# Four places for the last head's values, and a reordered lead-in with split gates in the experts

## The reference

```python
# cross attention, block 1
q = (inputs_q @ Wq).reshape(b, sq, H, HD) * (1.0 / np.sqrt(HD))      # H, HD = 16, 128
k = (inputs_kv @ Wk).reshape(b, skv, H, HD)                          # skv = 4096
v = (inputs_kv @ Wv).reshape(b, skv, H, HD)
attn = jax.nn.softmax(jnp.einsum('bqhd,bkhd->bhqk', q, k), axis=-1)
ctx = jnp.einsum('bhqk,bkhd->bqhd', attn, v).reshape(b, sq, H * HD)
return ctx @ Wo
# experts, block 6: E, K, F, C = 64, 8, 192, 64
probs = jax.nn.softmax(x @ router_w.T, axis=-1)
wts, idx = jax.lax.top_k(probs, K)
wts = wts / jnp.sum(wts, axis=-1, keepdims=True)
# each token goes to its 8 experts, at most 64 tokens an expert (xg: E x C x D)
h = jax.nn.silu(jnp.einsum('ecd,efd->ecf', xg, w1)) * jnp.einsum('ecd,efd->ecf', xg, v1)
y = jnp.einsum('ecf,efd->ecd', h, w2)
# out[token] = sum over its experts of y[expert, place] * weight
```

## Time and profile before

| | |
|---|---|
| median of 3 runs | 1778.88 us (1778.22 to 1780.69) |
| the profiled execution | 1774.9 us, its span 1772.9 us |
| PE busy | 1704.4 us (96%) |
| DVE, ACT, POOL busy | 1088.1 (61%), 693.3 (39%), 96.4 (5%) |
| the cross attention's last head | about 1164 to 1205 us |
| the experts' lead-in, the loop | about 1510 to 1546, then to the end |

### The profile page before, as it was taken

How to read it: one execution, slowest core, us unless ns; L and a number is a source line. 1 busy time by engine, 2 the same in 40 slices (tenths; PEclk the granted TensorE clock), 3 DMA queues, 4 the chain that set the end, 5 groups by cost and what they waited for, 6 DMA issues and landing times.

```text
span 1772.9 us, 23791 instructions
## 1 busy us (share of the span) xinstructions
PE 1704.4 (96%) x9438; PEld 1343.0 (76%) x9438; DVE 1088.1 (61%) x1738; ACT 693.3 (39%) x937; POOL 96.4 (5%) x177
## 2 busy tenths in 40 slices
PE   8998999999999999999999999978899999899998
PEld 7887888887888888788888788876577466554544
DVE  4446777777677777777777788965538315333333
ACT  4334444445444444444444555542213212212121
POOL 0000000000000000000000010010000000000000
PEclk9999999999999999999999999999999999999999
DMA  6755544445455454454454522252104181488880
GB/s 220 207 166 155 131 131 131 126 131 149 121 132 143 121 137 123 140 143 119 131 136 125 132 96 88 86 192 94 49 1 190 48 356 81 102 307 324 306 323 33
DMA packets 114733, 262.55 MB, mean 148 GB/s; under 512 B 6656, under 2 KB 76480, under 8 KB 108480
## 3 DMA queue, kind: packets, MB, share of 16 engines
q1 hardware_dynamic: 96192, 193.93, 35.5%
q0 software_dynamic: 18432, 67.12, 12.6%
HBM read 193.35 MB, written 67.67 MB: 147 GB/s over the span
## 4 chain that ended last, share of the span: by engine, by line
PE 64%; issue 24%; DVE 5%; DMA 3%; POOL 2%; ACT 1%; SPq 0%; POOLq 0%; DVEq 0%; ACTq 0%
PE bank L41 16%; PE bank L392 14%; PE bank L364 10%; PE bank L405 5%; PE bank L1712 5%; PE bank L1410 3%; PE bank L1733 2%; PE bank L1732 2%; PE bank L138 2%; PE bank L1741 2%; POOL v_back L867 1%; DMA v_dram<-v_out 1%; PE bank L1019 1%; DMA slot_all<-slots_dram 1%; PE bank L430 1%
## 5 line engine op out<-in xcount | busy, mean ns | idle before, releaser
L714 DVE TENSOR_TENSOR e_lo<-S,e_hi 128x1024 fp32r<-128x1024 f32 x128 | 156.6, 1223 | 94.1 <-ACT e_hi L547 93.8
L364 PE MATMUL bank<-cT_hi,wk_hi 128*128 128x512 f32 x512 | 205.6, 402 | 0.0
L392 PE MATMUL bank<-wv_hi,cT_hi 128*128 128x512 f32 x512 | 199.9, 390 | 3.5 <-DVE wv_lo L651 3.5
L364 PE MATMUL bank<-cT_hi,wk_lo 128*128 128x512 f32 x512 | 200.5, 392 | 0.0
L392 PE MATMUL bank<-wv_hi,cT_lo 128*128 128x512 f32 x512 | 199.4, 390 | 0.0
L364 PE MATMUL bank<-cT_lo,wk_hi 128*128 128x512 f32 x512 | 199.2, 389 | 0.0
L392 PE MATMUL bank<-wv_lo,cT_hi 128*128 128x512 f32 x512 | 199.2, 389 | 0.0
L538 ACT ACTIVATE S<-S 128x1024 f32<-128x1024 f32 x128 | 135.6, 1059 | 157.9 <-DVE S L694 157.8
L547 ACT CAST e_hi<-S 128x1024 fp32r<-128x1024 f32 x128 | 134.7, 1052 | 152.3 <-PE bank L405 142.7
L707 DVE TENSOR_TENSOR esum<-esum,S 128x512 f32<-128x512 f32 x210 | 145.1, 691 | 71.9 <-ACT S L538 68.3
L405 PE MATMUL bank<-e_hi,v_back 128*128 128x256 f32 x896 | 170.6, 288 | 12.2 <-DMA v_back<-v_dram 4.3
(11 more groups left out here) (265 smaller groups left out, 2899.8 us busy)
## 6 DMA issues: line engine op xcount, KB each, us to landing
w<-in_w_moe SPq DMA_DIRECT2D x32, 2304.0 KB, 8.5
v_dram<-v_out SPq DMA_DIRECT2D x112, 512.0 KB, 4.6
v_back<-v_dram POOLq DMA_DIRECT2D x112, 512.0 KB, 5.0
v_dram<-v_back SPq DMA_DIRECT2D x16, 512.0 KB, 3.9
v_late<-v_dram POOLq DMA_DIRECT2D x16, 512.0 KB, 3.5
ctx_nat<-in_ctx SPq DMA_DIRECT2D x8, 1024.0 KB, 4.6
ctx_raw<-in_ctxT SPq DMA_DIRECT2D x7, 1024.0 KB, 8.0
l_w_qkv<-in_l_wqkv SPq DMA_DIRECT2D x6, 1024.0 KB, 6.0
```

Source lines behind the costliest of these rows:

```text
L364: t = e.matmul(banks[b][:], l, r, start=(c == 0 and m == 0), stop=(c == DT - 1 and m == 2))
L392: t = e.matmul(banks[b][:], l, r, start=(c == 0 and m == 0), stop=(c == DT - 1 and m == 2))
L714: e.tensor_tensor(lo[:], Sj, hi[:].bitcast(F32), ALU.subtract).then_inc(e_split, 1)
```

## The change

In the last head (n from 120 on, `TAIL`) the values have four places: `v_back`, `v_late`, `v_tail0` (over the spare key tiles `k2_hi` and `k2_lo`) and `v_tail1` (over `wk_hi` and `wk_lo`), with a semaphore each. POOL issues rounds 1, 2 and 3 of that head together when head 14 is weighed, and later ones when the round four before is over. In the experts `slot` is turned before the first gathers; `xn_hi` and `xn_lo` are made before the logits are moved; `slotT` is copied before the gate weights are computed; `slot_all` is read in two pieces, four pairs first; and the gate weights are held as two float32r parts (`gate_parts`), so that a gate product has four columns in float32r instead of two in float32, and DVE adds the two halves when it moves the gates out of PSUM.

```diff
@@ -180,6 +180,10 @@
 
         ones_r, = place(WORK + 4 * (KVT * T + D), ("ones_r", [P, P], F32R))
 
+        TAIL = NH - NCH
+        v_tail0, = place(WV_PLACE + 4 * CT * 2 * XHD, ("v_tail0", [P, CT, 2, XHD], F32R))
+        v_tail1, = place(WORK + 4 * (KVT * T + D + DT * P), ("v_tail1", [P, CT, 2, XHD], F32R))
...
-        v_in = sems("v_in0 v_in1")
+        v_in = sems("v_in0 v_in1 v_in2 v_in3")
...
@@ -243,8 +247,9 @@
             late = n - LATE * NCH
             if late < 0:
                 return v_back, v_in[0], 16 * (n + 1)
-            b = late % 2
-            return (v_back, v_late)[b], v_in[b], 16 * (late // 2 + 1 + (LATE * NCH if b == 0 else 0))
+            b = late % 2 if n < TAIL else (n - TAIL) % 4
+            turns = late // 2 if n < TAIL else (TAIL - LATE * NCH) // 2 * (b < 2) + (n - TAIL) // 4
+            return (v_back, v_late, v_tail0, v_tail1)[b], v_in[b], 16 * (turns + 1 + (LATE * NCH if b == 0 else 0))
...
                 last = h // HPQ * KVT + CT * (j + 1) - 1
                 if n and late <= 0:
                     e.wait_ge(weighed, n)
+                elif n - TAIL in (2, 3):
+                    e.wait_ge(scored, NH)
+                    e.wait_ge(k_projected, NH)
+                elif n > TAIL + 1:
+                    e.wait_ge(weighed, n - 3)
                 elif late >= 2:
                     e.wait_ge(weighed, n - 1)
                 else:
@@ -882,8 +892,13 @@
                     elif n == LATE * NCH:
                         load_v(n)
                         load_v(n + 1)
-                    elif n + 1 < XH * NCH:
+                    elif n < TAIL:
                         load_v(n + 1)
+                    elif n == TAIL:
+                        for ahead in (1, 2, 3):
+                            load_v(n + ahead)
+                    elif n + 3 < NH:
+                        load_v(n + 3)
...
-        N_RING, EPP, GROUP = 7, 2, 4
+        N_RING, EPP, GROUP, FIRST = 7, 2, 4, 4
...
             e.dma_start(slots_dram, slotT[:]).then_inc(slots_out, 16)
             e.wait_ge(slots_out, 16)
             for s, rows in enumerate(halves):
-                e.dma_start(slot_all[rows], by_half[s].unsqueeze(0).to_broadcast([P // 2, PAIRS, T])).then_inc(slots_in, 16)
+                e.dma_start(slot_all[rows, 0:FIRST], by_half[s, 0:FIRST].unsqueeze(0).to_broadcast([P // 2, FIRST, T])).then_inc(slots_in, 16)
+            e.wait_ge(slots_in, 32)
+            for s, rows in enumerate(halves):
+                e.dma_start(slot_all[rows, FIRST:], by_half[s, FIRST:].unsqueeze(0).to_broadcast([P // 2, PAIRS - FIRST, T])).then_inc(slots_in, 16)
...
                     e.wait_ge(hid_moved, GROUP * g - 1)
                 for n in range(GROUP):
                     pair = slice(n * P, (n + 1) * P)
-                    two = slice(EPP * (GROUP * g + n), EPP * (GROUP * g + n + 1))
-                    t = matmuls(e, TURN_B[:, 2 * P + 2 * n:2 * P + 2 * n + 2],
-                                [(sel[:, g % 2, i, pair].bitcast(F32), gate_w[:, i, two]) for i in range(TT)])
+                    t = matmuls(e, TURN_B[:, 2 * P + 4 * n:2 * P + 4 * n + 4],
+                                [(sel[:, g % 2, i, pair], gate_parts[:, i, GROUP * g + n, :, :]) for i in range(TT)])
                 t.then_inc(gates_found, 1)
...
             stay_awake(e, GATHER_B, 7)
+            e.wait_ge(slot_made, 1)
+            for i in range(TT):
+                t = e.transpose(TURN_B[0:E, i * P:(i + 1) * P], slot[:, i, :], ident[:])
+            t.then_inc(slot_turned, 1)
             for c in range(DT):
                 gather(0, c)
-            e.wait_ge(slot_made, 1)
-            for i in range(TT):
-                t = e.transpose(TURN_B[0:E, i * P:(i + 1) * P], slot[:, i, :], ident[:])
-            t.then_inc(slot_turned, 1)
             find_gates(0)
...
             scalar_norm(e, 5)
+            e.copy(xn_hi[:], xn6[:]).then_inc(xn_rounded, 1)
             e.wait_ge(routed, TT)
             e.copy(logit[:].rearrange("p i n -> p (i n)"), banks[2][:, 0:TT * E]).then_inc(logits_moved, 1)
             for i in range(TT):
                 e.wait_ge(route_best, i + 1)
                 e.activation(raised6[:, i, :], logit[:, i, :], ACT.Exp, bias=route(i, 0)).then_inc(route_raised, 1)
-            e.wait_ge(ln_xn, TT * 6)
-            e.copy(xn_hi[:], xn6[:]).then_inc(xn_rounded, 1)
...
                 for s, rows in enumerate(halves):
-                    e.tensor_copy(gs[rows, g % 2, :], TURN_B[rows, 2 * P + s:2 * P + 2 * GROUP:2]).then_inc(gates_moved, 1)
+                    e.tensor_reduce(gs[rows, g % 2, :], TURN_B[rows, 2 * P + s:2 * P + 4 * GROUP:2].rearrange("p (n k) -> p n k", k=2),
+                                    AX.X, ALU.add).then_inc(gates_moved, 1)
...
                 if p == 0:
                     e.wait_ge(slots_in, 32)
                     e.wait_ge(consts_set, SLOTS_SET)
+                if p == FIRST:
+                    e.wait_ge(slots_in, 64)
                 if p >= 2:
...
             e.wait_ge(att_added, 2 * TT)
             vector_norm(e, 5, xn6)
+            e.wait_ge(xn_rounded, 1)
+            e.tensor_tensor(xn_lo[:], xn6[:], xn_hi[:].bitcast(F32), ALU.subtract).then_inc(xn_split, 1)
             e.wait_ge(logits_moved, 1)
             for i in range(TT):
                 own.done(e.max(route(i, 8, 16), logit[:, i, :]))
...
             make_sel(0)
-            e.wait_ge(xn_rounded, 1)
-            e.tensor_tensor(xn_lo[:], xn6[:], xn_hi[:].bitcast(F32), ALU.subtract).then_inc(xn_split, 1)
+            e.wait_ge(slot_turned, 1)
+            e.tensor_copy(slotT[:], TURN_B[0:E, 0:T]).then_inc(slot_moved, 1)
...
                 own.wait(e)
                 own.done(e.reciprocal(route(i, 2), route(i, 1)))
                 own.wait(e)
-                e.tensor_scalar(gate_w[:, i, :], gate_w[:, i, :], route(i, 2), None, ALU.mult).then_inc(route_gate, 1)
-            e.wait_ge(slot_turned, 1)
-            e.tensor_copy(slotT[:], TURN_B[0:E, 0:T]).then_inc(slot_moved, 1)
+                high, low_part = gate_parts[:, i, :, 0, :], gate_parts[:, i, :, 1, :]
+                gates = gate_w[:, i, :].rearrange("p (n s) -> p n s", s=EPP)
+                own.done(e.tensor_scalar(high, gates, route(i, 2), None, ALU.mult))
+                own.wait(e)
+                e.scalar_tensor_tensor(low_part, gates, route(i, 2), high.bitcast(F32), ALU.mult, ALU.subtract).then_inc(route_gate, 1)
             move_gates(0)
```

## The result

The changed kernel takes **1753.99 us** (median of 4 runs, 1752.51 to 1756.12) against 1778.55 (4 runs beside them, 1778.07 to 1780.69): 24.6 us less, a ratio of 0.9861 with the interval 0.9843 to 0.9878. The forecast was 1756.4, from 1752 to 1764.

What follows compares the result with a forecast made beforehand. PE, busy 96% of the span, was taken as the bound. Parts of -9.4, -7.2 and -5.9 sum to -22.5 us, from the median 1778.88 to 1756.4 us, range 1752 to 1764.

Steps and rivals of the forecast that it cites:

- Part A: Last cross-attention head: four places for values let rounds 2 to 7 run undisturbed by DMA waits, -9.4 us.
- even the worst row fits: Last head's value loads: the slowest landing, 7.1 us, stays within 7.4 us of cover, so no wait was taken.
- Rival 2: Last head: the value wait comes back in rounds 6 and 7, worth 3 us, giving 1759.4; chance 0.12.
- The rule weighed there: Last head's loads: DMA engines alternate between queues packet by packet; a small load takes about twice its undisturbed moving time.
- the wait at round 7: Last head: PE's wait for round 7's values, forecast to stay zero even beside a 1 MB weight load.
- Part B: Lead-in to the experts: earlier `slot` transposes, a full-clock first `up` and no `slot_all` wait, together -7.2 us.
- I take a full-clock `up`: Lead-in: the first `up` runs at full clock, 2.80 instead of 4.43 us, -1.6; bound on the other side 0.
- the stall of 2.81: Lead-in: PE's idleness before the second `turn`, behind the `slot_all` read; forecast to go whole, -2.8 us.
- The price of a late read: Lead-in: the short `slot_all` read comes as late as the long, costing 2.1 us; chance 0.08 shared with a clock fall.
- Part C: Expert loop: float32r gate products save 0.84 us in each of seven groups, -5.9 us; -4.6 by the 0.128 bound.
- Rivals 1, 4 and 5: Gate products: no cheaper, 1763.2 us (chance 0.12); fall to a quarter, 1753.0 (0.04); become dearer, 1783.7 (0.03).
- a change of length between 1205 and 1510: Unedited stretches between last head and lead-in: the forecast counted it as wrong if they did not keep their length.

## Why the prediction was right

**Part A** (-9.4; measured -9.49 + 0.53 = -8.96). That six rounds run undisturbed held: 2.58 us apart instead of 2.56, and head fell by 9.49 for the 9.46 laid out. Part of that closeness is luck: both are read from the same profile of before, the shortest of three with two places (43.93, 44.85, 45.56), so the four places save 9.5 to 11.1 us there. The step that failed is POOL's queue. I put 0.05 us on the two added issues, with "Issues take 0.53 us; three from 1161.52 end at 1163.1", three in a row without a gap. The profiles show a gap of 0.4 to 1.6 us ahead of the third, and `mrow` late by as much: by 0.54 us in the changed kernel's profile and 1.60 in its second one. It is paid in full, since every `shift` waits for `mrow`. That "even the worst row fits" held barely: in ten profiles with four places, loads of rounds 4 to 7 took 3.5 to 8.3 us, and three had a wait (1.11 us in round 7 with the whole read, 0.77 in round 6 with the late turn, 0.30 in round 7 with half the descriptor memory). Rival 2 was a real risk, at little more than a third of its price of 3 us. Its reason was too narrow: with the third weight asked for 4.7 us later, rounds 6 and 7 still landed in 6.2 and 6.3 us. A demand equal to what the engines move fits the numbers, and is not shown by an experiment. With three places the waits that the rival feared are there, 3.27 us.

**DMA turns.** The rule weighed there from the Trainium skill (DMA: Bandwidth & Descriptors, "Queues, rings and completion order") gave, as an estimate, about twice the undisturbed moving time for the small load. The landings of 6.0 to 8.3 us against 3.5 are 1.7 to 2.4 times as long, so the trace agrees in size. It does not test the rule, since further value loads were on the way in all of these; and the wait at round 7, which by the rule would stay at zero, was 1.11 and 0.30 us in two profiles.

**Part B** (-7.2; measured -7.85). The first `up` starts 10.81 us after the router instead of 13.99: -3.18 for -2.8, since the gathers start 0.26 us after the transposes and those 0.2 sooner than I had laid out (I began them at the end of the filler's record, and records overlap). The clock gave the -1.63 I took (4.43 to 2.80), with less certainty than "I take a full-clock `up`" sounds, as the third `up` of the variants shows; and the stall of 2.81 went whole. The price of a late read, 2.1, was 2.58 in the experiment, as PE is also sooner than I laid it out.

**Part C** (-5.9; measured -6.21). A group's chain row fell from 2.80 to 1.91, 0.89 instead of 0.84; seven times that is 6.23. A float32r product of 4 columns costs (1.91 - 1.12) / 8 = 0.10 us in the loop and 0.88 / 8 = 0.11 in the lead-in. The nearest row, the narrow float32 record of 0.105, was the right one, and the 256-column product of 0.128 was the bound. Rivals 1, 4 and 5 fall with it: one record costs what one record of the pair had cost, so the float32 product is two such, neither one nor four.

**The sum.** A, B and C measured are -23.0 us, for -22.5. What stands beside it, +1.5 and +1.4 us in stretches without an edit, is the scatter between executions. The prediction had named a change of length between 1205 and 1510 as a sign of being wrong; it came, and is no more than that scatter (308.7 to 310.6 us for the same code). Forecast 1756.4, median 1754.0: the medians fell by 24.6, 2.1 more than the sum forecast. Some of that may be the longer last head of before's other executions, which is not shown.

## What to carry to other kernels

A loop of rounds fed by loads is quick only if the cover of a load exceeds its landing while the other transfers run: here a cover of 7.4 us held in seven profiles of ten and cost 1.1 us at most in the others, and one of 4.9 cost 3.8 us. Before counting places, add up the bytes asked for per round over all queues and compare with what the busiest window of that stretch moved. Issues placed ahead of a collective on the same queue are paid by all who wait for it, so put the collective first (here 0.4 to 1.6 us). And a move of one step on one engine (the turn) is worth only what the order on the other engine (its copy) lets through: look at both queues before pricing it.

## What the runs showed of the hardware

- PE's granted clock fell from the upper level at the first `up` with idleness ahead of a long group (4.43 and 4.50 us, clock 0.62 and 0.59) and with 2.42 us of idleness ahead of a short one (4.50, clock 0.57), and stayed at 1.00 with 0.60 us ahead of a short group (2.80, twice, once with 1.32 us ahead of the gathers as well) or no idleness ahead of a long one (2.80). A wait of about 2.8 to 3 us before the third `up` was followed by a fall in one execution and by none in another.
- POOL's third load of 512 KB in a row begins 0.33 to 0.40 us after the first has landed, in seven of seven profiles, and directly in the one profile with the descriptor memory halved. The cause is open; a larger memory was not tried.
- In windows of 4 us in the last head the DMA engines moved 405 to 408 GB/s at most (share 1.1); they moved more elsewhere, 442 from 1548 to 1552 in the changed kernel at a share of 1.03, so 405 is not the most they can move with every kind of transfer. A 512 KB load took 3.5 us with few others on the way and 6 to 8.3 us among them.
